# Building the table of the loop's rounds in sub-blocks 2 to 11 in place of 0 to 4, in a graph and expert layer on one NeuronCore

## The reference

```python
xn  = layernorm(x)
agg = segment_sum(xn[src], dst, 1250) / max(count, 1)            # 40000 edges
gnn = relu(layernorm(xn @ w_self.T + agg @ w_neigh.T + bias) * gamma + beta)
q, k, v = split(xn @ w_qkv)                                       # 8 heads of 64
q_phi, k_phi = elu(q @ proj) + 1, elu(k @ proj) + 1
kv  = einsum('nhf,nhd->hfd', k_phi, v)
mix = (q_phi @ kv) / (q_phi . sum(k_phi)) @ w_proj + b_proj
x   = x + gnn + mix
x   = x + experts(layernorm(x))      # shared swiglu, top-2 of 8 experts, two groups
```

## Time and profile before

| | us |
|---|---|
| median of three runs | 750.01 |
| lowest and highest of them | 749.41, 750.44 |
| the profiled execution, its own time | 746.69 |
| its span in the profile | 744.7 |

### The profile page before, as it was taken

How to read it: one execution, slowest core, us unless ns; L and a number is a source line. 1 busy time by engine, 2 the same in 40 slices (tenths; PEclk the granted TensorE clock), 3 DMA queues, 4 the chain that set the end, 5 groups by cost and what they waited for, 6 DMA issues and landing times.

```text
span 744.7 us, 12041 instructions
## 1 busy us (share of the span) xinstructions
PE 708.5 (95%) x4382; PEld 433.8 (58%) x4382; DVE 386.4 (52%) x735; ACT 261.9 (35%) x386; POOL 174.4 (23%) x170
## 2 busy tenths in 40 slices
PE   6989899997999999998999999999889999999998
PEld 5646577774576656565756644446745555555554
DVE  5874678964476757876246422222235523441154
ACT  4853123323652231356353123333336443532000
POOL 3340000000061000013222257742312212222362
PEclk9999999998999999999999999999999999999999
DMA  9200002000031150011325212222166766643675
GB/s 249 96 1 1 1 2 114 2 13 2 1 138 61 29 198 1 0 28 28 114 84 169 56 28 58 58 79 92 29 227 239 264 216 239 230 136 130 195 211 150
DMA packets 24417, 73.90 MB, mean 99 GB/s; under 512 B 7059, under 2 KB 7405, under 8 KB 20274
## 3 DMA queue, kind: packets, MB, share of 16 engines
q1 hardware_dynamic: 8607, 39.74, 15.8%
q0 software_dynamic: 10768, 25.52, 11.6%
q10 hardware_dynamic: 4994, 8.01, 2.9%
HBM read 57.90 MB, written 15.31 MB: 98 GB/s over the span
## 4 chain that ended last, share of the span: by engine, by line
PE 77%; DVE 11%; ACT 6%; issue 3%; DMA 3%; DVEq 0%; POOL 0%; SPq 0%; ACTq 0%; POOLq 0%
PE banks L1343 59%; PE banks L1392 6%; PE banks L1380 3%; PE banks L1701 3%; DMA y_rows<-xT 2%; DVE st L768 1%; PE banks L1572 1%; PE banks L1366 1%; ACT W L435 1%; DMA x<-in_x 1%; PE banks L1581 1%; DVE xn L1154 1%; DVE W L745 1%; PE banks L1373 1%; ACT big L612 1%
## 5 line engine op out<-in xcount | busy, mean ns | idle before, releaser
L1343 PE MATMUL banks<-W,xT 128*125 128x512 f16 (+1 forms) x1392 | 318.2, 383 | 8.0 <-ACT xT L710 2.2
L1343 PEld LDWEIGHTS banks<-W,xT 128*125 128x125 f16 (+2 forms) x1392 | 165.3, 122 | 137.4 <-issue 15.9
L1343 PE MATMUL banks<-xT,W 128*128 128x500 f16 (+1 forms) x720 | 131.0, 344 | 1.8 <-DVE xn L1293 1.4
L1343 PEld LDWEIGHTS banks<-xT,W 128*128 128x128 f16 x720 | 70.7, 99 | 60.5 <-issue 4.4
L745 DVE SCALAR_TENSOR_TENSOR W<-stg,W 128x2048 f16<-128x2048 f32 x30 | 68.5, 2304 | 40.9 <-ACT W L435 40.9
L1343 PE MATMUL banks<-W,big 128*125 128x512 f16 x360 | 81.5, 380 | 0.0
L1343 PEld LDWEIGHTS banks<-W,big 128*125 128x125 f16 x360 | 48.3, 136 | 29.2 <-issue 2.3
L377 POOL DMA_INDIRECT xn<-h_rows,tokidx x29 | 35.3, 1217 | 125.1 <-PE banks L1701 114.7
L366 POOL TENSOR_TENSOR big<-xn,big 125x512 f16<-125x512 f32 x20 | 23.5, 1173 | 174.7 <-ACT big L627 174.7
L1313 DVE CAST xT<-banks 128x1024 f32 x22 | 26.9, 1222 | 69.0 <-PE banks L1701 69.0
L435 ACT ACTIVATE W<-stg 128x2048 f16<-128x2048 f32 x30 | 56.4, 1903 | 0.0
(11 more groups left out here) (324 smaller groups left out, 785.0 us busy)
## 6 DMA issues: line engine op xcount, KB each, us to landing
stg<-in_units SPq DMA_DIRECT2D x30, 1024.0 KB
y_rows<-xT ACTq DMA_DIRECT2D x29, 256.0 KB
h_rows<-big POOLq DMA_DIRECT2D x10, 500.0 KB, 3.6
out_x<-x SPq DMA_DIRECT2D x10, 224.0 KB
stg<-in_wqkT SPq DMA_DIRECT2D x2, 1024.0 KB, 11.0
x<-in_x SPq DMA_DIRECT2D x2, 896.0 KB
xn<-h_rows,tokidx POOLq DMA_INDIRECT x29, 5.3
x<-in_x SPq DMA_DIRECT2D x1, 448.0 KB
```

The source lines that it names most:

```text
L1343: ins = te.matmul(dst, lhs(sl, c), rhs(sr, c), start=(first and c == 0 and k == 0), stop=(last and c == n - 1 and k == 2))
```

## The change

The steps of the table move to later sub-blocks, on both engines: `outside` from 0 to 2 (with a new wait for its own last reduction), `outside_rows` from 1 to 5, the copy from 2 to 7, the masks from 3 to 9 and the table from 4 to 11 on DVE; the sum from 1 to 4, the turns from 2 to 6, the prefix sum from 3 to 8 and the two sums from 4 to 10 on PE. Their results go to bank 5 in place of 4 and bank 6 in place of 5, since bank 4 now holds block 0's spread meanwhile. PE waits for `tab_rdy` no longer ahead of the counts of `g` = 5, but ahead of the spread in `g` = 10, which is the first to write bank 5. A row of 400 numbers (`items_io`) lies in `gcat` in place of `big`. The first two folds move from 12 and 15 to 14 and 16. And on ACT `rows_high` of tiles 8 and 9 moves from ahead of `key_phi(5)` to behind it.

```diff
-FOLD_AT = {12: 4, 15: 5, 18: 6, 21: 7}
+FOLD_AT = {14: 4, 16: 5, 18: 6, 21: 7}
...
-        items_io = big[0:NBLK, 0:2 * EXTRA].bitcast(F32)
+        items_io = gcat[0:NBLK, 3 * DIM:3 * DIM + EXTRA]
...
             key_phi(4)
-            for t in range(5, TILES):
+            for t in range(5, 8):
                 rows_high(t)
             key_phi(5)
+            rows_high(8)
+            rows_high(9)
             value_out(0)
...
-                if g == 0:
-                    key_sum(7)
+                if g < 2:
+                    key_sum(7 + g)
+                if g == 2:
                     outside()
-                if g == 1:
+                    dve.wait_ge(S["vi_red"], 1)
+                if g == 5:
                     dve.wait_ge(S["ex_row"], 1)
                     outside_rows()
-                    key_sum(8)
-                if g == 2:
+                if g == 7:
                     dve.wait_ge(S["ex_col"], 1)
-                    v.tensor_copy(scr[0:NBLK, 2632:2634], ps[4][0:NBLK, 0:2]).then_inc(S["ex_col"], 1)
-                if g == 3:
+                    v.tensor_copy(scr[0:NBLK, 2632:2634], ps[5][0:NBLK, 0:2]).then_inc(S["ex_col"], 1)
+                if g == 9:
                     extras_masks()
-                if g == 4:
+                if g == 11:
                     extras_table()
...
-                if g == 5:
-                    pe.wait_ge(S["tab_rdy"], 1)
                 count_windows(j // 2, j % 2, g % RING)
-                if g == 1:
+                if g == 4:
                     pe.wait_ge(S["vi_red"], 1)
-                    te.matmul(ps[4][0:1, 192:192 + NSUB], ones[0:80, 0:1], ...).then_inc(S["vi_row"], 1)
-                if g == 2:
+                    te.matmul(ps[5][0:1, 192:192 + NSUB], ones[0:80, 0:1], ...).then_inc(S["vi_row"], 1)
+                if g == 6:
                     pe.wait_ge(S["ex_row"], 2)
...
-                if g == 3:
+                if g == 8:
                     pe.wait_ge(S["ex_col"], 2)
...
-                if g == 4:
+                if g == 10:
                     pe.wait_ge(S["ex_sum"], 1)
-                    te.matmul(ps[5][0:1, 0:EXTRA], ones[0:NBLK, 0:1], mk1, start=True, stop=True)
-                    te.matmul(ps[4][0:1, 0:EXTRA], ones[0:NBLK, 0:1], mk0, ...).then_inc(S["ex_sum"], 1)
+                    pe.wait_ge(S["k_rel"], TILES)
+                    te.matmul(ps[6][0:1, 0:EXTRA], ones[0:NBLK, 0:1], mk1, start=True, stop=True)
+                    te.matmul(ps[5][0:1, 0:EXTRA], ones[0:NBLK, 0:1], mk0, ...).then_inc(S["ex_sum"], 1)
                 if i:
                     if j == 0:
                         pe.wait_ge(S["ct_rdy"], 3 * i)
+                        if i == 2:
+                            pe.wait_ge(S["tab_rdy"], 1)
                     part = spread((i - 1) % 2, range(2 * j, 2 * j + 2), i - 1)
...
                 if g in FOLD_AT:
-                    if g == 12:
+                    if FOLD_AT[g] == 4:
                         pe.wait_ge(S["ld_wq"], 16)
                         pe.wait_ge(S["k_rel"], TILES)
```

More of the change, by code:

```diff
@@ L915, in outside @@
                 link(v.tensor_tensor(w, tnum4.unsqueeze(1).to_broadcast([80, NSUB, 4]),
-                                     ps[4][0:80, 128:128 + NSUB].unsqueeze(2).to_broadcast([80, NSUB, 4]), ALU.subtract))
+                                     ps[5][0:80, 128:128 + NSUB].unsqueeze(2).to_broadcast([80, NSUB, 4]), ALU.subtract))
                 link(v.tensor_scalar(w, w, 0.0, float(SUB - WIN), ALU.max, ALU.min))
@@ L925, in outside_rows @@
                 dve.wait_ge(S["vi_row"], 1)
-                link(v.tensor_reduce(again, ps[4][0:1, 192:192 + NSUB].rearrange("p (b j) -> p b j", j=SUBS), AX.X, ALU.max))
+                link(v.tensor_reduce(again, ps[5][0:1, 192:192 + NSUB].rearrange("p (b j) -> p b j", j=SUBS), AX.X, ALU.max))
                 link(v.tensor_scalar(again, again, 1.0, None, ALU.min))
@@ L935, in extras_masks @@
                 dve.wait_ge(S["ex_pre"], 1)
-                link(v.tensor_copy(sx, ps[4][0:NBLK, 0:1]))
+                link(v.tensor_copy(sx, ps[5][0:NBLK, 0:1]))
                 link(v.tensor_tensor(se, sx, scr[0:NBLK, 2632:2633], ALU.add))
@@ L950, in extras_table @@
                 v.memset(tab[0:1, ITEMS:ITEMS + 1], NBLK - 1)
-                v.tensor_copy(tab[0:1, 1:ITEMS], ps[5][0:1, 0:EXTRA])
-                v.tensor_copy(tab[0:1, ITEMS + 1:2 * ITEMS], ps[4][0:1, 0:EXTRA])
+                v.tensor_copy(tab[0:1, 1:ITEMS], ps[6][0:1, 0:EXTRA])
+                v.tensor_copy(tab[0:1, ITEMS + 1:2 * ITEMS], ps[5][0:1, 0:EXTRA])
                 link(v.tensor_reduce(scr[0:1, 2640:2641], rounds, AX.X, ALU.add))
@@ L1472, in _ @@
             pe.wait_ge(S["vi_dg"], 1)
-            te.matmul(ps[4][0:80, 128:128 + NSUB], ones[0:NSUB, 0:80], scr[0:NSUB, 2700:2700 + NSUB], start=True, stop=True).then_inc(S["vi_bc"], 1)
+            te.matmul(ps[5][0:80, 128:128 + NSUB], ones[0:NSUB, 0:80], scr[0:NSUB, 2700:2700 + NSUB], start=True, stop=True).then_inc(S["vi_bc"], 1)
             values_mm(3)
@@ L1480, in _ @@
                     pe.wait_ge(S["ct_rdy"], 3 * (i - 1) + j // 2 + 1)
-                if g == 5:
-                    pe.wait_ge(S["tab_rdy"], 1)
                 count_windows(j // 2, j % 2, g % RING)
-                if g == 1:
+                if g == 4:
                     pe.wait_ge(S["vi_red"], 1)
-                    te.matmul(ps[4][0:1, 192:192 + NSUB], ones[0:80, 0:1], scr[0:80, 2460:2460 + NSUB], start=True, stop=True).then_inc(S["vi_row"], 1)
-                if g == 2:
+                    te.matmul(ps[5][0:1, 192:192 + NSUB], ones[0:80, 0:1], scr[0:80, 2460:2460 + NSUB], start=True, stop=True).then_inc(S["vi_row"], 1)
+                if g == 6:
                     pe.wait_ge(S["ex_row"], 2)
-                    te.matmul(ps[4][0:NBLK, 0:1], scr[0:1, 2610:2610 + NBLK], one[0:1, 0:1], start=True, stop=True)
-                    te.matmul(ps[4][0:NBLK, 1:2], scr[0:1, 2620:2620 + NBLK], one[0:1, 0:1], start=True, stop=True).then_inc(S["ex_col"], 1)
-                if g == 3:
+                    te.matmul(ps[5][0:NBLK, 0:1], scr[0:1, 2610:2610 + NBLK], one[0:1, 0:1], start=True, stop=True)
+                    te.matmul(ps[5][0:NBLK, 1:2], scr[0:1, 2620:2620 + NBLK], one[0:1, 0:1], start=True, stop=True).then_inc(S["ex_col"], 1)
+                if g == 8:
                     pe.wait_ge(S["ex_col"], 2)
-                    te.matmul(ps[4][0:NBLK, 0:1], tri[0:NBLK, 0:NBLK], scr[0:NBLK, 2632:2633], start=True, stop=True).then_inc(S["ex_pre"], 1)
-                if g == 4:
+                    te.matmul(ps[5][0:NBLK, 0:1], tri[0:NBLK, 0:NBLK], scr[0:NBLK, 2632:2633], start=True, stop=True).then_inc(S["ex_pre"], 1)
+                if g == 10:
                     pe.wait_ge(S["ex_sum"], 1)
-                    te.matmul(ps[5][0:1, 0:EXTRA], ones[0:NBLK, 0:1], mk1, start=True, stop=True)
-                    te.matmul(ps[4][0:1, 0:EXTRA], ones[0:NBLK, 0:1], mk0, start=True, stop=True).then_inc(S["ex_sum"], 1)
+                    pe.wait_ge(S["k_rel"], TILES)
+                    te.matmul(ps[6][0:1, 0:EXTRA], ones[0:NBLK, 0:1], mk1, start=True, stop=True)
+                    te.matmul(ps[5][0:1, 0:EXTRA], ones[0:NBLK, 0:1], mk0, start=True, stop=True).then_inc(S["ex_sum"], 1)
                 if i:
```

## The result

| | median, us | runs | range, us |
|---|---|---|---|
| before | 748.05 | 20 | 742.28 to 753.88 |
| the changed kernel | 751.95 | 20 | 748.36 to 757.31 |

The ratio is 1.0055, with a 95% interval of 1.0034 to 1.0076: 0.55% slower, about 4.1 us, where the prediction had 3.8 us. (Ratios leave out a run that lies over 1.5% above the fastest of its own kernel.) The profiled execution of the changed kernel took 754.0 us, with a span of 751.9 and a mean granted clock of 0.983; it lies 2 us above its median, and that of before 1.4 us under its own, so the two spans differ by 7.2 us, more than the kernels do.

What follows compares the result with a forecast made beforehand. PE was taken as the bound, busy 95% of the span. Old gap -3.98 us, new gaps +4.9, small steps +0.3 and clock +2.6 gave +3.8, a median of 753.8 us; range 749.5 to 756.5.

Steps and rivals of the forecast that it cites:

- The old gap goes, a new one of 3.4 us comes ahead of `g` = 10: PE's cost at `g` = 4, 3.98 us with slowed matmuls, vanishes; PE waits 3.4 us for windows before counts of 10.
- A second gap of 1.46 us ahead of the spread: In `g` = 10, PE stands 1.46 us before the spread, which writes bank 5 and waits for `tab_rdy`.
- The sum without new clock, +1.2 us: At the spread of `g` = 10: -3.98, +4.9 for the gaps, +0.3 for three small steps, giving +1.2 us.
- the lower bound given: Spread of `g` = 10 only 0.8 us later, with the small steps hidden and the masks started 0.2 us earlier.
- The clock, +2.6 us, as one stretch and a half: Behind the new gaps, one 1.2 GHz stretch of 1.7 us plus half a second, 0.9; bounds 0 to 4.0.
- the rival with the thin sums at the low level: Three low stretches, or both sums of 1 x 400 taking 2.9 us instead of 1.43: +6, 756.0; chance 0.13.
- The total: Whole kernel +3.8 us: +1.2 without clock and +2.6 for the clock; median 753.8 us.
- A gap of this length brings a fall: PE idle times of 2.29, 3.17 and 2.09 us each preceded the 1.2 GHz level; one of 2.00 did not.
- The relu is worth 0: On ACT, relu ends 1.06 us earlier, but the wait at turn L1459 grows from 0.77 to 1.8: worth 0.
- Folds, banks, data, the own wait: 0: Moved folds worth 0, at worst 0.7 us; bank numbers and `items_io` free; own reduction's wait costs DVE 0.2 us.
- The rival on the faster side: DVE three windows ahead at `g` = 9, so PE's work covers the masks: -2.2 us, 747.8; chance 0.08.
- the tie that I named: At `g` = 8, DVE is held to PE's counts, which it can't pass, so masks start at 91.15.

Runs made afterwards that it cites:

- the first four experiments: Kernel before with relu order alone, 0.9995; changed kernel with old ACT order, 1.0067; kernel before with folds alone, 0.9994; changed kernel with tile 9's values in sub-block 9, 1.0013.

## Why the prediction was right

Point by point, by its own steps.

- *The old gap goes, a new one of 3.4 us comes ahead of `g` = 10.* It was 3.21. The counts of `g` = 10 were put at 96.7 and started at 96.28. The 0.4 us come from ahead of it: taking the three small steps out from ahead of the counts of `g` = 4 let these start at 80.47 in place of 81.44, where I had taken 80.9, and everything up to the gap stood 0.4 us earlier. The step that carried the forecast was that the masks' 5.54 us are a fixed block and only its cover changes; moving tile 9's values under it showed that.
- *A second gap of 1.46 us ahead of the spread.* 1.48, and it went with the bank.
- *The sum without new clock, +1.2 us.* It was too high. At the full clock the spread of `g` = 10 would start at 96.28 + 3.43 = 99.71, and with both gaps filled it did start at 99.83, against 98.95 before: 0.8 to 0.9 us later, the lower bound given. The time of that kernel, +0.17% or 1.3 us, is too wide (-0.8 to +3.4) to decide it.
- *The clock, +2.6 us, as one stretch and a half.* The profiled execution shows more: the spread began at 101.49 in place of 99.71, and from there to the values of tile 9 it was 107.20 - 101.49 = 5.71 us in place of 102.76 - 98.95 = 3.81, together 3.7 us. On the mean, filling the gaps won 0.38%, 2.8 us, and the bounds of 0 and 4.0 held. This one execution shows the rival with the thin sums at the low level, which had 0.13: they took 2.8 us in place of 1.43, and the low level went on to 105.4. The profile with the table alone has the same ten microseconds (96.7 to 106.9). How often it comes in the other runs is not known.
- *The total.* So in the profile the sum was 0.76 in place of 1.2 and the clock 3.7 in place of 2.6, together 4.4 in place of 3.8. That the total came so near the measured 4.1 is partly luck: the mechanism was as forecast, the two sizes erred to opposite sides.
- *A gap of this length brings a fall.* This was the weak step. I read three of three off one trace, and a gap of 2.00 us without a fall as a bound. Over the 14 profiles the gap of 3.17 us was followed by the low level in all 13 that have it, the one of 2.29 in 3 of 3 (for 3.4, 6.8 and 6.8 us), but the one of 2.09 in only 5 of 13, and the one of 2.00 in 3 of the 5 kernels that still had it. Nor does it take 2 us: behind the two gaps of 1.51 and 1.36 us that all 14 have between 526 and 544 us, a low stretch began in 10, and near 210 us in 4 with no gap over 0.7 beside it. The sentence that I weighed (the Trainium skill, "TensorE: Matmul & The Clock Gate", section on what is actually happening: the watching runs on a clock of its own that doesn't start with the kernel) fits the 5 of 13 and the 3 of 5, against the row.
- *The relu is worth 0.* On the chain it is: 0.98 at the relu and 1.79 at the turn, as worked out. Missed was that with the gap of 2.00 us cut to 0.98, and the later one grown from 0.77 to 1.79, the falls there are gone from the profiles: 0 of the 9 profiles with the new order show the low level between 40 and 50 us, against 3 of the 5 with the old. At 1.7 us a stretch that would be some 1 us on the mean; the time (0.9995, with 0.0027 to either side) doesn't settle it.
- *Folds, banks, data, the own wait: 0.* The folds alone are at 0.9994, and no other wait turned up.
- *Cover for the masks.* The rival on the faster side did not come in: the masks started at 90.68, reckoned 91.15. What held them was not quite the tie that I named. The prefix sum of `g` = 8 was done at 90.53, and DVE came to the masks at 90.68 without idling, straight from two windows; it had last waited, for 2.17 us, at the copy for PE's turns of `g` = 6. Further ahead it could have won only 0.15 us, since it can't pass the prefix sum.

## What to carry to other kernels

Where two engines hand a chain to and fro inside a stream, put what the other engine wants next ahead of each link in the queue, and lay the other engine's long work over the longest link: the same chain cost PE 4 us (reckoned from the trace of before), 8 us (4.1 more, measured) or next to nothing (3.5 us less than before, measured), by its place alone. More steps between the links are no cover if the steps there are short: count cover in microseconds. And a wait that only guards a bank is a link too.

## What the runs showed of the hardware that I had not expected

- Much of the spread between executions goes with TensorE's clock. Of the kernel before, beside the first four experiments, the run with a mean granted clock of 0.995 took 743.1 us, those at 0.986 took 748.2 to 750.0, and the one at 0.981 took 752.3. Over the 95 runs of that kernel beside all the experiments, time and mean granted clock have a correlation of -0.91, though at 0.991 alone the times run from 743.4 to 747.8. A single profile can lie several microseconds off the median with nothing changed.
- Matmuls whose results nobody needs, put into a gap of 2.3 us, made a kernel 0.33% faster (0.9943 to 0.9991).
- The low level can begin inside a gap and outlast it by nine microseconds, as it did from 95.2 to 105.4 over a gap that ended at 96.28, with the thin sums and a second gap behind it. With dense matmuls in both gaps there was none from 92 to 106.
